# A four-layer transformer on one core: how the rope attentions fill their operand stack, and how far the second score pass runs behind the first

## The reference, cut to what matters

```
Q, K = rope(x @ W_q), rope(x @ W_k)          # 16 heads x 8 features
V = x @ W_v
scores = Q @ K.T / sqrt(8), masked above the diagonal
out = softmax(scores) @ V @ W_o              # 256 x 256 scores per head
```

## Time and profile before

| | us |
|---|---|
| median of 3 executions | 3025.16 (3025.08 to 3026.27) |
| the profiled execution | 3025.41 |
| its span in the trace | 3023.7 |
| rope attention of phase 4, barrier to last matmul | 1925.9 to 2256.2 |
| rope attention of phase 6, the same | 2494.0 to 2812.5 |
| TensorE busy, whole span | 2683.4 (89%) |
| granted clock of TensorE, mean | 0.927 |

### The profile page before, as it was taken

The page is one execution under the profiler, slowest core; times in us unless marked ns, Lnnn a source line. Parts: engine busy times, 40 slices in busy tenths (PEclk is TensorE's granted clock), DMA queues, the critical chain, the costliest instruction groups (busy, mean ns, idle before and its releaser), DMA issues. The chain is left out here.

```text
span 3023.7 us, 67058 instructions
## 1 busy us (share of the span) xinstructions
PE 2683.4 (89%) x21108; PEld 2309.7 (76%) x21108; DVE 2218.1 (73%) x6616; ACT 1444.7 (48%) x4145; POOL 579.4 (19%) x1032
## 2 busy tenths in 40 slices
PE   6999999998999899999998999579976765999786
PEld 5988888897888799999997999456654543666565
DVE  4888888886776477777776777457759985777797
ACT  3666666665555466666663223135542221545321
POOL 0000000000111000000000111167751214776111
PEclk9999999999999999999998999789995556999899
DMA  5000000002000544444441000222220002222000
GB/s 137 2 2 1 1 1 1 1 1 59 1 0 4 157 151 146 147 147 146 146 151 31 1 0 0 88 73 75 72 59 8 0 0 78 75 72 68 1 0 28
DMA packets 137064, 160.83 MB, mean 53 GB/s; under 512 B 9360, under 2 KB 127520, under 8 KB 135832
## 3 DMA queue, kind: packets, MB, share of 16 engines
q1 hardware_dynamic: 136856, 158.43, 17.8%
HBM read 92.32 MB, written 64.96 MB: 52 GB/s over the span
## 5 line engine op out<-in xcount | busy, mean ns | idle before, releaser
L134 POOL TENSOR_TENSOR hT<-hT 128x256 fp32r<-128x256 f32 x64 | 46.8, 731 | 1470.5 <-ACT hT L127 1470.5
L118 PE MATMUL bank<-hT,a_xA 128*128 128x256 f32 x768 | 228.3, 297 | 5.7 <-ACT a_p L429 3.0
L572 DVE TENSOR_REDUCE a_nmax<-bank 128x2 f32<-128x512 f32 x256 | 174.9, 690 | 58.3 <-PE bank L120 56.2
L119 PE MATMUL bank<-hT,a_xA 128*128 128x256 f32 x768 | 217.4, 283 | 0.0
L120 PE MATMUL bank<-hT,a_xA 128*128 128x256 f32 x768 | 216.9, 282 | 0.0
L1647 ACT ACTIVATE a_p<-bank 128x1024 f32<-128x1024 f32 (+1 forms) x256 | 193.4, 808 | 23.3 <-PE bank L1703 19.2
L1021 ACT ACTIVATE a_p<-a_p,a_nmax 128x256 f32<-128x256 f32 x256 | 128.1, 501 | 135.1 <-DVE a_nmax L1205 135.1
L450 ACT CAST a_xA<-bank 128x256 fp32r<-128x256 f32 x256 | 94.8, 372 | 200.8 <-PE bank L120 200.8
L1286 ACT ACTIVATE f_silu<-bank 128x512 f32<-128x512 f32 x128 | 76.5, 597 | 214.6 <-PE bank L120 214.5
L814 PE MATMUL bank<-arena,f_hidden 128*128 128x128 f32 x1024 | 171.6, 288 | 6.3 <-DVE f_acc L868 5.0
L751 ACT ACTIVATE f_hidden<-bank,arena 128x256 f32<-128x256 f32 x256 | 120.3, 472 | 114.4 <-PE bank L120 113.1
(11 more groups left out here) (287 smaller groups left out, 8584.3 us busy)
## 6 DMA issues: line engine op xcount, KB each, us to landing
pos_dram<-a_pos SPq DMA_DIRECT2D x128, 383.0 KB
a_shifted<-pos_dram SPq DMA_DIRECT2D x128, 256.0 KB, 2.7
cut_dram<-a_cut SPq DMA_DIRECT2D x64, 192.0 KB, 3.8
a_stack<-cut_dram SPq DMA_DIRECT2D x128, 96.0 KB
gate<-gates_dram SPq DMA_DIRECT2D x8, 1024.0 KB, 17.2
a_stack<-cut_dram SPq DMA_DIRECT2D x128, 64.0 KB
arena<-in_task SPq DMA_DIRECT2D x1, 4624.0 KB, 14.3
a_stack<-cut_dram SPq DMA_DIRECT2D x128, 32.0 KB
```

The source lines that it names most:

```text
L118: pe.matmul(out, left[0], right[0], start=start, stop=False, skip_group_check=True)
L119: pe.matmul(out, left[0], right[1], start=False, stop=False, skip_group_check=True)
L572: dve.tensor_reduce(nmax[:, at.ring(2), h, :], s_ps[h][:].rearrange("p (t k) -> p t k", t=NT), AX_X, ALU.max, negate=True).then_inc(s["nma ...
```

## The change

It has four parts, all of them in how data is brought in, and one in the order of steps.

1. `load_gate` issues four DMAs of four rows each in place of one of sixteen, in every phase. `task` is loaded by four DMAs. In the rope attentions the loads for the next phase aren't issued at the start any more but one piece a step, from step 0 of item 0 on.
2. The three parts of k are written to DRAM by three DMAs, each as soon as it is cut; q still by one. The tensors `cut_q` and `cut_k` are laid out so that a half of the stack is filled by two DMAs: 75 rows of q (25 source rows, each three times, the last a row of zeros) and 72 rows of k (24 source rows, three times over). The stack thus holds all nine products of parts where it held six.
3. `scores_by_key` runs three steps behind `scores` and `values` four, where they ran four and five behind. ACT's copy of the summed values moves from p = 1 to the start of p = 0.
4. At the start DVE doesn't zero a part of the stack any more (POOL zeroes both), and it fills `v` with its constants only after the first q was rotated. TensorE waits for the rows of ones before its first score, not before its first matmul.

```diff
+GATE_PIECES = 4
+PIECES = {"task": 4}
...
 def load_gate(sp, k, phase):
-    sp.dma_start(k.gate[phase % 2][:], k.gates_dram[:, phase, :].partition_broadcast(P)).then_inc(k.gate_in[phase], 16)
+    for g in range(GATE_PIECES):
+        load_gate_piece(sp, k, phase, g)
...
@@ def rope_attention
-    ROWS = DH * sum(PARTS - a for a in range(PARTS))
+    ROWS = DH * PARTS * PARTS
+    QROWS = DH * PARTS + 1
-    FILLS = 2 * PARTS + 1
+    FILLS = 2
...
             def _(sp):
-                prefetch(sp, nc, k, d, phase)
+                def prefetch_piece(s):
+                    if 0 <= s < weight_pieces(phase + 1):
+                        load_weight_piece(sp, k, d, phase + 1, s)
+                    if 0 <= s - weight_pieces(phase + 1) < GATE_PIECES:
+                        load_gate_piece(sp, k, phase + 1, s - weight_pieces(phase + 1))
...
                 def fill(at, half):
-                    for which in range(2):
-                        row = 0
-                        for a in range(PARTS):
-                            rows = (PARTS - a) * DH
-                            start = (place(at) * PARTS * 2 + (1 if which else 2 * a)) * ROW + 8 * half * T
-                            src = bass.AP(cut_dram.tensor, start,
-                                          [[2 * ROW if which else 0, PARTS - a], [H * T, DH], [1, 8 * T]])
-                            sp.dma_start(stack[row:row + rows, place(at), which, heads].rearrange("r h t -> r (h t)"),
-                                         src).then_inc(sem, 16)
-                            row += rows
-                    sp.dma_start(stack[ROWS:ROWS + SHIFTS, place(at), 0, heads], constant_rows(zeros, 8)).then_inc(sem, 16)
+                    q_rows = bass.AP(cut_q.tensor, place(at) * QROWS * H * T + 8 * half * T,
+                                     [[H * T, QROWS], [0, PARTS], [1, 8 * T]])
+                    k_rows = bass.AP(cut_k.tensor, place(at) * (QROWS - 1) * H * T + 8 * half * T,
+                                     [[0, PARTS], [H * T, QROWS - 1], [1, 8 * T]])
+                    sp.dma_start(stack[0:ROWS + PARTS, place(at), 0, heads].rearrange("r h t -> r (h t)"), q_rows
+                                 ).then_inc(sem, 16)
+                    sp.dma_start(stack[0:ROWS, place(at), 1, heads].rearrange("r h t -> r (h t)"), k_rows
+                                 ).then_inc(sem, 16)
...
                 def write(at, which):
-                    wait(sp, s["cut"], at, 10, 5 - 5 * which, item=True)
-                    sp.dma_start(cut_dram[place(at), :, which].rearrange("a r t -> r a t"), cut[:, :, which]
-                                 ).then_inc(written[which], 16)
+                    if which:
+                        for a, done in enumerate((6, 9, 10)):
+                            wait(sp, s["cut"], at, 10, 10 - done, item=True)
+                            k_rows = bass.AP(cut_k.tensor, (place(at) * (QROWS - 1) + a) * H * T,
+                                             [[PARTS * H * T, DH], [T, H], [1, T]])
+                            sp.dma_start(k_rows, cut[:, a, 1]).then_inc(written[1], 16)
...
+                    if isinstance(at.base, int) and at.base == 0:
+                        prefetch_piece(at.s)
...
             def _(pe):
-                pe.wait_ge(s["ones_in"], 32)
...
-                    b4, b5 = at.shift(-4), at.shift(-5)
+                    b3, b4 = at.shift(-3), at.shift(-4)
...
-                    if b4.real:
-                        scores_by_key(b4)
+                    if b3.real:
+                        scores_by_key(b3)
...
-                    if b5.real:
-                        values(b5)
+                    if b4.real:
+                        values(b4)
```

More of the change, by code:

```diff
@@ L297, in load_gate, with load_gate_piece, weight_pieces, load_weight_piece @@
 def load_gate(sp, k, phase):
[L299 to L302 removed]
+    for g in range(GATE_PIECES):
+        load_gate_piece(sp, k, phase, g)
+def load_gate_piece(sp, k, phase, g):
+    n = NB // GATE_PIECES
+    sp.dma_start(k.gate[phase % 2][:, g * n:(g + 1) * n], k.gates_dram[g * n:(g + 1) * n, phase, :].partition_broadcast(P)
+                 ).then_inc(k.gate_in[phase], 16)
+def load_weights(sp, nc, k, d, phase):
+    for piece in range(weight_pieces(phase)):
+        load_weight_piece(sp, k, d, phase, piece)
+def weight_pieces(phase):
+    return sum(PIECES.get(name, 1) for name, _, _ in WEIGHTS[phase])
+def load_weight_piece(sp, k, d, phase, piece):
     at = 0
     for name, shape, parts in WEIGHTS[phase]:
[L306 to L307 removed]
+        size, cuts = int(np.prod(shape)), PIECES.get(name, 1)
+        if 0 <= piece < cuts:
+            part = size // cuts
+            whole = d[name]
+            if cuts > 1:
+                whole = whole[:, piece * part:(piece + 1) * part]
+            sp.dma_start(k.arena[phase % 2][0:parts, at + piece * part:at + (piece + 1) * part], whole
+                         ).then_inc(k.weights_in[phase], 16)
+        piece -= cuts
         at += size
@@ L1574, in cut_up @@
                     wait(pool, terms_ready, at, item=True)
-                    wait(pool, written[which], at.shift(-PER), 16, item=True)
+                    wait(pool, written[which], at.shift(-PER), 16 * PARTS if which else 16, item=True)
                     x, y, c = terms[:, which, 0, :], terms[:, which, 1, :], cut[:, :, which, :]
@@ L1617, in step @@
                     ni, ni2, pi = at.shift(PER), at.shift(2 * PER), at.shift(-PER)
-                    pi2, b4 = at.shift(-2 * PER), at.shift(-4)
+                    pi2, b3 = at.shift(-2 * PER), at.shift(-3)
+                    if at.p == 0 and pi2.real:
+                        wait(act, s["o_mm"], pi2.shift(3))
+                        wait(act, s["back_mm"], pi2.shift(-PER), item=True)
+                        act.copy(o[:], o_ps[:]).then_inc(s["o"], 1)
                     if at.p == 0 and pi.real:
@@ L1642, in step @@
                         act.copy(oT[:], misc_ps[:, 0:T]).then_inc(s["oT"], 1)
-                    if b4.real:
-                        wait(act, s["o_mm"], b4.shift(-2))
+                    if b3.real:
+                        wait(act, s["o_mm"], b3.shift(-2))
                         for part, (first, end) in enumerate(((0, 4 * T), (4 * T, 6 * T))):
-                            wait(act, s["sT_mm"], b4, 2, 1 - part)
-                            act.activation(p[:, b4.ring(2), first:end], sT_ps[:, first:end], ACT.Exp
+                            wait(act, s["sT_mm"], b3, 2, 1 - part)
+                            act.activation(p[:, b3.ring(2), first:end], sT_ps[:, first:end], ACT.Exp
                                            ).then_inc(s["exp"], 1)
@@ L1673, in scores @@
                 def scores(at):
+                    if isinstance(at.base, int) and at.base == 0 and at.s == 0:
+                        pe.wait_ge(s["ones_in"], 32)
                     if at.p % 2 == 0:
```

101 lines of the change are left out of this document (54 added, 47 removed).

## The result

The changed kernel takes 3175.93 us (median of four, 3168.84 to 3178.79), the kernel before 3025.72 beside it (3025.08 to 3027.16). The ratio is 1.0492, with a 95% interval of 1.0474 to 1.0511. The forecast was slower, by 63 us, with a range to 3125; it is slower by 150.

The account below looks back on a forecast made before the run. The prediction took TensorE to bound the rope attentions now, and a ring of waits through shift and fill after the change. 3023.7 - 35.3 (start) + 68 (lap) + 30 (pieces) = 3086.4, 3088 with 1.7 around the span; range 3010 to 3125 us.

Parts of the forecast that it names:

- What bounds the kernel: In the long run of the rope attentions (phases 4 and 6) TensorE is the bound, a lap taking 16.67 us.
- the mechanism: In phases 4 and 6 the first scores_by_key waits once a lap for shift_rows, queued behind a fill; 2.4 us.
- the sign: Whole kernel: slower than before, given a chance of 0.78.
- The start: Starts of phases 4 and 6: less TensorE wait for the ones, -23.4 and -11.9, together -35.3 us, firm to 2.
- The pieces: Loads for the next phase now stand among the fills in phases 4 and 6: +30 us, bounds 0 and 44.
- the 1.5 us to start and the 1.6 for `base`: Amounts taken off `task`'s 14.3 us load time to price one of its pieces at 2.8 us.
- The lap: One item in phases 4 and 6: 19.1 us against 16.67, 2.4 more, over 14 laps in each phase +68 us.
- I count nothing for the clock: TensorE's waits of 2.4 us a lap in phases 4 and 6 were given no cost for a lower clock.
- the ring: Waits from scores_by_key through k's rotation, cuts, DRAM write and fill to the next scores_by_key; one turn 19.1 us.
- the fill leg: From a fill's issue to the shift's landing: 8.3 us before, 0.8 more for five more rows, so 9.1.
- the rival "worse": Waits of 2.4 us bring the clock down, or q runs on few engines: above 3125 us; chance 0.06.
- The 2.0 us plus bytes at 436 GB/s: Skill's DMA fit: 600 KB would take 3.4 us, no bound; the prediction said the trace disagrees, 400 KB taking 8.3.

Follow-up runs that it names:

- experiment 2: Kernel before, with only scores_by_key three steps behind scores and values four (ACT's copy moved to match): 3145.88 us, ratio 1.0413.
- experiment 3: Changed kernel with fills on twelve engines: q as 72 rows, k as three DMAs of 24 rows, zeros by a fifth: 3004.06 us, ratio 0.9949.
- experiment 9: Changed kernel with q alone spread over twelve engines (72 rows, two rows of zeros by a third DMA), k unchanged: 3129.34 us, ratio 1.0354.
- experiment 8: Changed kernel with the old seven-DMA fill and old lags of four and five steps; load pieces and new start kept: 3020.60 us, ratio 0.9992.
- experiment 5: Changed kernel with 14 added matmuls keeping TensorE busy before the wait for an item's first shift: 3136.94 us, ratio 1.0373.
- experiment 1: Changed kernel with the lags alone undone, scores_by_key four steps behind scores and values five: 3075.73 us, ratio 1.0181.
- experiment 7: Changed kernel with fills on twelve engines and scores_by_key four steps behind scores again: 2988.05 us, ratio 0.9879.

## Why the prediction was wrong

- **What bounds the kernel, the mechanism, the sign: right.** The lap closes through `shift_rows` behind the fill, the wait stands where it was put, and q runs on few engines. Experiments 2, 3 and 9 show it: the lag of three alone brings it, the rows per engine set it, a wide fill removes it. Three engines for k and five for q fit the shares of 0.19 and 0.29 in the windows above.
- **The start: right within 3 us.** The first transposes come at 1932.45 for a forecast 1930.6, TensorE waits 10.9 us instead of 33.7, and in phase 6 10.7 instead of 21.9, 2.7 more than forecast. By the trace the 2 us missing are DVE behind POOL (last section). By the first `scores` less is left: 1978.22 - 1959.92 = 18.3 us in phase 4 where 23.4 were forecast; 2.4 of the difference are the new first fill, 10.7 us (issued at 1949.25) where the old one took 8.3. "Firm to 2 us" was too firm.
- **The pieces: right in sum with the start, which may be luck.** Start and pieces were -35 and +30; experiment 8, which has just these two, measured 0 to -5. No run has the pieces alone, and no row shows the 1.5 us to start and the 1.6 for `base` in their price; `base` landed 3.9 us after its issue in the kernel before. In the changed kernel all that isn't the long laps of the next point comes to 149.1 - 149.4, about zero.
- **The lap: the step that failed.** It read 19.1 against 16.67, +68; measured are 22.3 and 21.7, so 14 x 5.64 + 14 x 5.03 = +149.4. Of the 3.2 us a lap missing in phase 4, 2.0 are "I count nothing for the clock". I had taken a wait of 2.4, near the 1.87 after which TensorE went on at full pace, and put the clock at nothing. That was wrong for the very wait that I forecast: in experiment 2 waits of 2.4 to 3.3 us already have the low clock behind them (0.67 after 2.52) and a leg of 5.0 instead of 3.3. In the changed kernel waits of 3.0 to 5.0 bring some 5 us mostly at the lower level; these are in the ring and so make the wait no shorter. It is experiment 5 that shows that the clock makes the leg long. Another 0.9 are in the fill leg, 10.0 for 9.1. Against experiment 2 the new fill has 0.95 more, where I had 0.8 for its rows, and experiment 2 has 0.8 more than the phase's first fill, which I had taken as the price of a fill in a lap. How much of this 0.8 is the one more DMA in that leg, and how much the traffic of a lap, is open.
- **The range.** Its upper end came from laps of up to 20; the rival "worse" named the clock and got 0.06 (0.05 where the range is worked out). Its price was there: 1.6 to 2 us more in a leg of 3.3 that TensorE fills, times 28, is the step from 3088 to over 3130.
- **A second ring wasn't seen.** Fill, fill, write, fill on the same engines closes at 18 to 20 us with lag four (experiment 1). In the changed kernel the longer one should hide it, so it changed no number of the forecast, but my expectation of experiment 1.
- **A fit that wasn't for these DMAs.** The 2.0 us plus bytes at 436 GB/s that the prediction quotes stand in that page of the Trainium skill (DMA: Bandwidth & Descriptors) under "Anatomy of one DMA — SWDGE (gpsimd) path" and are for DMAs that GpSimd issues. All fills here are issued by SP, so the 8.3 us of a fill say nothing against it. No term of the sum used it.
- **Does it add up?** Lag three alone costs 125 us (2), the new fill alone 55 (1 against 8), start and pieces nothing (8), and all together 150: two rings that share the fill, of which the longer counts.

## What to carry to other kernels

Write down each ring of waits with its legs before taking slack out of it, and the rings that run only through a DMA queue too; compare them with the lap of the bounding engine. A step of lag that looks idle can be what keeps a ring open. Once the ring makes TensorE wait, a leg that TensorE itself fills has to be priced at its lower clock level too. Over the 5 us behind a wait, the mean granted clock was full after 1.46 (experiment 1) and 1.87 us. It was 0.50 to 0.70 after each of the waits of 2.4 to 5.0 us in the long laps of experiment 2 and of the changed kernel; one wait of 2.67 in experiment 7 left it full. And look at how many engines a DMA runs on: a mean DMA share of 0.25 hid fills that ran on two or three, and nearly the same bytes in five issues on twelve engines each made the program 5% faster than two issues on five and three.

## What was unexpected in the hardware

- **DVE stood behind POOL's zeroing.** POOL zeroes both places now. DVE and POOL at the start of phase 4:

```profile
1925.14 7.02 POOL L1610 MEMSET a_stack<- 128x4096 f32 x2 [1.29 <-POOLq L89]
...
1925.76 0.20 DVE L146 TENSOR_TENSOR row_m<-row_stats 128x32 f32<-128x32 f32 x1
1925.99 2.70 DVE L148 TENSOR_SCALAR row_mean<-row_mean 128x32 f32<-128x32 f32 x1
...
1929.63 2.68 DVE L171 TENSOR_SCALAR xn<-x,row_mean,row_rstd 128x128 f32<-128x128 f32 x2
```

  The operation of L148 in the kernel before, and the normalisation there in the earlier trace rows, 0.47 for two:

```profile
1931.01 0.18 DVE L144 TENSOR_SCALAR row_mean<-row_mean 128x32 f32<-128x32 f32 x1
```

  Both long ones end where one of POOL's two memsets of 3.5 us ends (1928.7 and 1932.2), while operations that combine two tiles, as that of L146, run at their usual pace beside it. The Trainium skill (SBUF — State Buffer, "SBUF: two separate sides") says that a pair of ports is shared by DVE and GpSimd (POOL) as an exclusive lock for the whole instruction, which DVE needs for operations in a 2-port mode, and for two SBUF inputs only against a GpSimd operation that reads SBUF, which a memset doesn't; the trace agrees with that. No run here took POOL's zeroing away, so that it is the cause isn't shown by an experiment.
- **A pause of TensorE in experiment 5.** Once, with nothing that the trace shows to wait for, it stood 5.35 us:

```profile
2139.86 0.58 PE L1729 MATMUL bank<-a_stack 128*128 128x128 bf16 x4 [5.35 <-issue]
```

  The cause is open; it is 5 of that kernel's 3137 us.
